# Another order of the steps of a fused decoder layer, on every engine of the core

## The chip, the core and the metric

The kernel runs on one core of a Trainium2 chip. A core has five engines with a queue of instructions each: TensorE (PE in the profile; PEld is its loading of weights), VectorE (DVE), ScalarE (ACT), GpSimd (POOL) and SyncE (SP), which here issues all DMAs. Each engine works off its own queue strictly in order, and waits at an instruction until the semaphores that it names have reached their values. The metric is the time of one execution on the device in microseconds (us); of several runs the median is given.

## What is computed

A decoder layer in float32 over 8 sequences (batches) of 256 tokens with 128 channels: linear attention, causal cross attention to a context, and a feed-forward part with routed experts and a short convolution. Each part takes a layer norm of its input and adds its output to it.

```python
def layer(x, ctx):                       # (8, 256, 128) each
    x = x + attn(layernorm(x))           # 16 heads of 8; phi(t) = elu(t) + 1
    x = x + xattn(layernorm(x), ctx)     # 16 heads of 8, causal softmax
    return x + ffn(layernorm(x))

def attn(x):
    q, k, v = split(x @ Wqkv.T); q, k = phi(q), phi(k)
    kv, k_sum = einsum('bnhd,bnhm->bhdm', k, v), k.sum(1)
    return (q @ kv / (q @ k_sum + 1e-6)) @ Wproj.T + bproj

def xattn(x, ctx):
    q, k, v = x @ Wq.T, ctx @ Wk.T, ctx @ Wv.T
    return softmax(where(causal, q @ k.T / sqrt(8), -inf)) @ v @ Wo.T

def ffn(x):                              # scores: 8 experts, two chosen
    scores = sigmoid(x @ Wr); cw = weights_of_top2(scores + router_bias)
    routed = sum(cw[e] * ((silu(x @ Wg[e]) * (x @ Wu[e])) @ Wd[e]) for e in range(4))
    routed += (cw[4] + cw[6]) * x + cw[7] * relu(x)
    return routed + causal_conv4(x, conv_w) + conv_b
```

## The kernel before

The eight batches go through the same steps, and the steps of up to four batches are mixed, so that every engine has work while others wait. A step is a Python function that issues a few instructions on one engine with the waits they need; the table `ORDER` at the head of the file lists for each engine its steps as `name.batch.number`, and `program` issues them in that order. Nothing else orders the work: neither the tiles nor the eight PSUM banks are chosen by it.

The steps, by the names that the texts below use:

- Linear attention: `stats1`, `var1` (DVE), `rstd1` (POOL, two instructions at L480 and L488), `norm1` (POOL at L498; DVE for batches 0 and 1), `self_x_t` (PE transposes), `xnT` (ACT copy), `self_q1`, `self_kv` (PE), `act_q`, `act_kv` (ACT), `phi_q`, `phi_k` (DVE), `self_sum` (PE), `kvsum` (DVE), `self_out` (PE), `div1` (DVE, three parts), `self_o_t` (PE), `o1T` (ACT), `self_proj` (PE), `x1` (DVE, adds what POOL's `bias` made). They go through `self_bank`, for batches 1 and 2 through `pv_bank` and `ffn_bank`.
- Cross attention, its operands: `stats2` to `norm2`, `cross_norm_t`, `x2nT`, `cross_q2` for q, `cross_k_v` for k and v. q and k are split into three bfloat16 parts, `hi` and `mid` (ACT), `rest` (DVE), `lo` (POOL), which SP's DMAs stack into `qs` and `ks`.
- Cross attention, its maxima: for each batch six units, `max.b.0` to `max.b.5` on PE write scores to the pair of banks `max_pair`, and `reduce` (DVE, L839) takes the maxima from it. There is one such pair, so a `max` waits for the `reduce` before it. After three units `maxrow` (PE) transposes the maxima, `max_hi` (ACT) and `max_mid` (DVE) split them, and `send_max` (SP) moves them into `qs`.
- Cross attention, softmax: `soft` (PE, six units, through `soft_pair`) needs the maxima; `exp` (ACT), `mask` (POOL, L524), `pv` (PE, two halves of three masks each), `outT`, `out_t`, `div2` (DVE), `o2_t`, `o2T`, `o_proj` (PE), `x2` (DVE).
- Feed-forward: `stats3` to `shift3` (DVE) and `norm3` (ACT, L606), `ffn_x_t`, `x3T`, `ffn_router`, `tanh_r`, `sig`, `route` (DVE, seven parts), `ffn_gate_up` (PE, two halves), `tanh_g` (ACT), `gate` and `times_up` (DVE), `hid` (POOL), `ffn_hid_t`, `hidT`, `tap` (convolution), `ffn_down` (PE, twelve products, needs `hidT` and all taps), `skip`, `relu7`, `base` (POOL), `finish` (DVE), `store_out`.

## Time and profile before

| | us |
|---|---|
| median of 3 runs (196.34 to 197.08) | 196.93 |
| the profiled execution | 196.06 |
| its span on the core | 194.3 |
| DVE busy | 163.4 |
| PE busy | 166.0 |
| ACT busy | 124.9 |
| POOL busy | 113.8 |

The span reaches from the first to the last instruction. An engine's busy time is the time in which it worked on an instruction; PE's ends are modelled. Of the views, the windows give busy times of a stretch, the timeline the instructions in order with the idle time before each and what ended it, and the granted clock is the share of TensorE's full speed. In the timelines steps of one name can be told apart by their tiles (`negmax<-max_pair` is a `reduce`) and by their time.

### The profile page before, as it was taken

Reading aid. Unit: us, or ns where it says so; the run is one execution under the profiler, and the core shown is the slowest. Engines: PE = TensorE matmul, PEld = TensorE weight load, DVE = VectorE, ACT = ScalarE, POOL = GpSimd, SP = SyncE. Lnnn points to the kernel's source line nnn. Section 1 sums busy time; section 2 is a strip of 40 time slices with the busy share of each in tenths; the row PEclk is TensorE's granted clock in tenths of the full one; section 3 lists DMA queues with packets and bytes.
Section 4 is the critical chain, followed back from the end, with each engine's and each line's share of the span. In section 5 each row is a group of like instructions: output and inputs, shape, how many; then the busy total and the mean of one; then the engine's idle time right before and its main releaser. Section 6 shows DMA issues by size and latency. Waiting matters only on the chain.

```text
span 194.3 us, 5501 instructions
## 1 busy us (share of the span) xinstructions
PE 166.0 (85%) x1812; PEld 114.5 (59%) x1812; DVE 163.4 (84%) x458; ACT 124.9 (64%) x281; POOL 113.8 (59%) x204
## 2 busy tenths in 40 slices
PE   6958697778898899995999999988988998797973
PEld 6846484545566556672866576656646546554542
DVE  6665878847787889998999989999999799399893
ACT  2036563528857798785776398858976568756560
POOL 7864877951932873798236633657366167754432
PEclk9999999969999999999999999999999999999999
DMA  5931131120332210013203211232121000000001
GB/s 174 321 142 41 36 84 48 46 69 15 97 83 57 59 32 21 1 46 107 71 4 83 60 48 31 55 86 57 44 59 33 27 7 2 27 3 0 30 2 54
DMA packets 17796, 11.00 MB, mean 57 GB/s; under 512 B 2388, under 2 KB 17108, under 8 KB 17768
## 3 DMA queue, kind: packets, MB, share of 16 engines
q1 hardware_dynamic: 17768, 10.66, 18.7%
q8 instruction: 14, 0.23, 0.5%
q14 instruction: 14, 0.11, 0.2%
HBM read 3.10 MB, written 1.05 MB: 21 GB/s over the span
## 4 chain that ended last, share of the span: by engine, by line
DVE 29%; PE 23%; issue 21%; POOL 18%; ACT 6%; DVEq 1%; POOLq 0%; ACTq 0%
DVE negmax L839 7%; PE max_pair L966 4%; POOL rstd L488 4%; POOL xn L498 4%; PE ffn_bank L966 4%; PE self_bank L966 4%; PE pv_bank L966 4%; DVE convT L944 3%; ACT probs L641 3%; POOL probs L524 2%; DVE stats L735 2%; PE soft_pair L966 2%; POOL hid L533 2%; POOL vareps L480 1%; POOL xres L506 1%
## 5 line engine op out<-in xcount | busy, mean ns | idle before, releaser
L839 DVE TENSOR_REDUCE negmax<-max_pair 128x4 f32<-128x1024 f32 (+1 forms) x48 | 58.5, 1218 | 6.6 <-PE max_pair L966 6.1
L641 ACT ACTIVATE probs<-soft_pair 128x1024 f32<-128x1024 f32 x48 | 49.0, 1020 | 8.8 <-PE soft_pair L966 8.8
L524 POOL TENSOR_SCALAR_AFFINE_SELECT probs<-probs 128x512 f32<-128x512 f32 (+1 forms) x48 | 37.5, 795 | 21.8 <-ACT probs L641 21.8
L966 PE MATMUL pv_bank<-probs,vs 128*32 128x128 f32 (+1 forms) x512 | 23.7, 328 | 1.6 <-POOL probs L524 1.4
L966 PEld LDWEIGHTS pv_bank<-probs,vs 128*32 128x32 f32 x512 | 14.4, 109 | 10.6 <-POOL probs L524 3.7
L966 PE MATMUL soft_pair<-qs,ks 64*128 64x256 bf16 (+1 forms) x256 | 18.9, 247 | 1.1 <-ACT probs L641 1.0
L966 PE MATMUL max_pair<-causal,picks 64*128 64x128 bf16 (+1 forms) x192 | 15.5, 240 | 4.8 <-DVE negmax L839 3.2
L606 ACT ACTIVATE xn<-x,shift,rstd 128x128 f32<-128x128 f32 x32 | 14.0, 488 | 8.4 <-DVE shift L759 8.4
L966 PE MATMUL max_pair<-ks,qs 64*128 64x128 bf16 (+1 forms) x256 | 18.8, 245 | 0.0
L488 POOL TENSOR_TENSOR rstd<-vareps,exponent 128x2 f32<-128x2 f32 x24 | 17.4, 725 | 2.0
L533 POOL TENSOR_TENSOR hid<-hraw,cw 128x256 f32<-128x256 f32 x16 | 10.3, 649 | 13.6 <-DVE hraw L921 7.1
L966 PE MATMUL ffn_bank<-loaded,x3T 128*128 128x8 f32 (+1 forms) x52 | 17.0, 423 | 0.6 <-ACT x3T L667 0.5
L944 DVE SCALAR_TENSOR_TENSOR convT<-x3T,loaded,convT 128x256 f32<-128x256 f32 x24 | 15.3, 638 | 0.2
L966 PEld LDWEIGHTS max_pair<-causal,picks 64*128 64x128 bf16 x192 | 6.1, 95 | 14.2 <-DVE negmax L839 8.4
L966 PEld LDWEIGHTS soft_pair<-qs,ks 64*128 64x128 bf16 x256 | 8.7, 94 | 9.8 <-ACT probs L641 5.9
L480 POOL TENSOR_SCALAR vareps<-mv 128x2 f32<-128x2 f32 x24 | 5.5, 230 | 12.7 <-DVE mv L749 11.4
L514 POOL TENSOR_TENSOR qparts<-qrest,qparts 128x256 bf16<-128x256 f32 x8 | 5.6, 703 | 8.7 <-ACT qparts L623 8.7
L548 POOL TENSOR_TENSOR base<-skip,relu 128x256 f32<-128x256 f32 x8 | 6.0, 750 | 7.3 <-DVE skip L936 4.0
L966 PEld LDWEIGHTS max_pair<-ks,qs 64*128 64x128 bf16 x256 | 10.0, 95 | 0.3
L498 POOL TENSOR_SCALAR xn<-loaded,mv,rstd 128x128 f32<-128x128 f32 x12 | 9.5, 799 | 0.1
L966 PEld LDWEIGHTS ffn_bank<-loaded,x3T 128*128 128x128 f32 x52 | 7.3, 190 | 2.6 <-ACT x3T L667 1.3
L966 PE MATMUL cross_bank<-loaded 128*128 128x128 f32 (+1 forms) x48 | 8.6, 316 | 0.1
(195 smaller groups left out, 386.8 us busy)
## 6 DMA issues: line engine op xcount, KB each, us to landing
ks<-kparts SPq DMA_DIRECT2D x48, 64.0 KB, 2.0
qs<-qparts SPq DMA_DIRECT2D x48, 64.0 KB, 2.1
out_dram<-result SPq DMA_DIRECT2D x8, 128.0 KB, 1.8
loaded<-packed_dram SPq DMA_DIRECT2D x1, 768.0 KB, 7.7
loaded<-packed_dram SPq DMA_DIRECT2D x1, 640.0 KB, 8.8
qs<-maxparts SPq DMA_DIRECT2D x32, 4.0 KB
loaded<-packed_dram SPq DMA_DIRECT2D x1, 462.5 KB, 6.3
...
```

Source lines behind the costliest of these rows:

```text
L480: nc.gpsimd.tensor_scalar(t["vareps"][:, :], t["mv"][b.par][:, :, 1], 1.0, 1e-5, ALU.mult, ALU.add).then_inc(vareps_done[n], 1)
L488: nc.gpsimd.tensor_tensor(t["rstd"][b.par][:, :], t["vareps"][:, :], exponent[:, :], ALU.pow).then_inc(rstd_done[n], 1)
L498: nc.gpsimd.tensor_scalar(t["out"][b.par][:, i, :], x_of(b)[:, i, :], t["mv"][b.par][:, i, 0:1], t["rstd"][b.par][:, i:i + 1], ALU.subtrac ...
L514: nc.gpsimd.tensor_tensor(parts[n][b.par][:, 2, :], rest[n][b.par][:, :], parts[n][b.par][:, 1, :], ALU.subtract).then_inc(lo_done[n], 1)
L524: nc.gpsimd.affine_select(out=v, in_=v, compare_op=ALU.is_ge, fill=0.0, base=0, pattern=[[0, n], [1, P]], channel_multiplier=-1).then_inc( ...
L533: nc.gpsimd.tensor_tensor(hid[b.par][:, t, :].rearrange("p (e i) -> p e i", e=EM), hid0[:, t, :].rearrange("p (e i) -> p e i", e=EM), cw[b ...
L548: nc.gpsimd.tensor_tensor(base[b.par][:, :, :], skip[b.par][:, :, :], relu7[b.par][:, :, :], ALU.add).then_inc(base_done, 1)
L606: nc.scalar.activation(t["out"][b.par][:, i, :], source[:, i, :], ACT.Identity, bias=t["shift"][b.par][:, i:i + 1], scale=t["rstd"][b.par] ...
L641: nc.scalar.activation(probs[b.par][g][:, k, :], soft_pair[:, :], ACT.Exp).then_inc(exp_done, 1)
L839: nc.vector.tensor_reduce(maxima, max_pair[:, :].rearrange("p (u h k) -> p u h k", u=2, h=n), AX.X, ALU.max, negate=True).then_inc(max_rea ...
L944: nc.vector.scalar_tensor_tensor(out=convT[b.par][:, :], in0=x3T[b.par][:, j:j + S], scalar=w["conv"][:, j:j + 1], in1=convT[b.par][:, :], ...
L966: return nc.tensor.matmul(out, lhsT, rhs, start=start, stop=stop, skip_group_check=True)
```

## The change

The table `ORDER` is replaced by another for all five engines, found with shorter occupancies (the time that a step is taken to hold its engine) for the groups of TensorE. The steps, their instructions, tiles and banks are the same. The new table is a line shorter, so POOL's code stands one line higher in the file. One wait is new, in ACT's `norm3`; the diff shows it with a line of the table for POOL and for PE.

```diff
 ORDER = {
...
     "pool": """
...
-        mask.0.5 lo_k.3.0 mask.1.0 mask.1.1 mask.1.2 rstd3.0.0 rstd1.6.0 mask.1.3 rstd2.4.0 mask.1.4 lo_q.3.0
...
+        lo_k.2.0 lo_k.3.0 rstd1.6.0 norm1.5.0 norm1.6.0 rstd3.0.0 bias.6.0 mask.1.0 lo_q.3.0 mask.1.1 mask.1.2
...
     "pe": """
...
-        self_out.3.0 max.0.1 cross_q2.1.0 max.0.2 self_o_t.3.0 cross_k_v.2.0 maxrow.0.0 self_proj.3.0 max.0.3
...
+        max.0.1 cross_q2.1.0 self_out.3.0 max.0.2 cross_k_v.2.0 maxrow.0.0 max.0.3 self_o_t.3.0 self_proj.3.0
...
                         if n == 3:
                             act.wait_ge(skip_done, b.count(2, -2))
+                            act.wait_ge(relu7_done, b.count(2, -2))
```

Three places of the order follow, two on PE and one on POOL.

PE, batch 0's linear attention between `self_sum.0` (`vones0,phik0`) and `self_proj.0` (`o1T0` into `self_bank`). `ident,xn1_0` into `ffn_bank` are the transposes of batch 2, `kvsum0,phiq0` is `self_out.0`, `ident,o10` is `self_o_t.0`. Before:

```order
L966 MATMUL self_bank<-vones0,phik0 128x144 x2
L970 MATMUL pv_bank<-ident,xn1_1 128x128 x2
L970 MATMUL ffn_bank<-ident,xn1_0 128x128 x2
L966 MATMUL self_bank<-kvsum0,phiq0 128x144 x2
L966 MATMUL pv_bank<-xnT1,loaded 128x256
L966 MATMUL ffn_bank<-xnT0,loaded 128x256
L970 MATMUL self_bank<-ident,o10 128x128 x2
L966 MATMUL pv_bank<-loaded,xnT1 128x256 x2
L966 MATMUL self_bank<-loaded,o1T0 128x128 x2
```

Now:

```order
L966 MATMUL self_bank<-vones0,phik0 128x144 x2
L970 MATMUL pv_bank<-ident,xn1_1 128x128 x2
L966 MATMUL self_bank<-kvsum0,phiq0 128x144 x2
L966 MATMUL pv_bank<-xnT1,loaded 128x256
L970 MATMUL ffn_bank<-ident,xn1_0 128x128 x2
L970 MATMUL self_bank<-ident,o10 128x128 x2
L966 MATMUL ffn_bank<-xnT0,loaded 128x256
L966 MATMUL self_bank<-loaded,o1T0 128x128 x2
```

`self_out.0` and `self_q1.1` have moved ahead of batch 2's transposes, and `self_proj.0` ahead of `self_kv.1`.

PE, between `max.0.3` (the first two rows) and `max.0.5` (the last `causal,picks` and `ks0,qs0`). `ident,xn1_0` into `self_bank` is `self_x_t.4`, `ident,xn2_0` is `cross_norm_t.2`, the single `soft_pair` row `soft.0.0`. Before:

```order
L966 MATMUL max_pair<-causal,picks 128x4x64 x4
L966 MATMUL max_pair<-ks0,qs0 128x128 x8
L970 MATMUL cross_bank<-ident,xn2_0 128x128 x2
L970 MATMUL self_bank<-ident,xn1_0 128x128 x2
L966 MATMUL max_pair<-causal,picks 128x2x64 x4
L966 MATMUL max_pair<-ks0,qs0 128x256 x4
L966 MATMUL cross_bank<-x2nT0,loaded 128x256
L966 MATMUL self_bank<-xnT0,loaded 128x256
L966 MATMUL soft_pair<-qs0,ks0 128x256 x4
L966 MATMUL max_pair<-causal,picks 128x2x64 x4
L966 MATMUL max_pair<-ks0,qs0 128x256 x4
```

Now:

```order
L966 MATMUL max_pair<-causal,picks 128x4x64 x4
L966 MATMUL max_pair<-ks0,qs0 128x128 x8
L970 MATMUL self_bank<-ident,o11 128x128 x2
L966 MATMUL self_bank<-loaded,o1T1 128x128 x2
L966 MATMUL max_pair<-causal,picks 128x2x64 x4
L966 MATMUL max_pair<-ks0,qs0 128x256 x4
L970 MATMUL self_bank<-ident,xn1_0 128x128 x2
L966 MATMUL soft_pair<-qs0,ks0 128x256 x4
L970 MATMUL cross_bank<-ident,xn2_0 128x128 x2
L966 MATMUL max_pair<-causal,picks 128x2x64 x4
L966 MATMUL max_pair<-ks0,qs0 128x256 x4
```

`max.0.4` has moved ahead of the transposes of batches 2 and 4, `soft.0.0` too, and `cross_q2.2` and `self_q1.4` behind `max.0.5`.

POOL, from `lo_k.3` (`kparts1`) on. `probs10` and `probs11` are masked in `mask.1.0` to `mask.1.5`, `rstd3_0` is `rstd3.0`, `xn1_1` and `xn1_0` are `norm1.5` and `norm1.6`. Before:

```order
L514 TENSOR_TENSOR kparts1<-krest1,kparts1 128x256
L524 AFFINE_SELECT probs10<-probs10 128x4x128 x2
L524 AFFINE_SELECT probs10<-probs10 128x1024
L480 TENSOR_SCALAR vareps3<-mv3_0 128x2
L488 TENSOR_TENSOR rstd3_0<-vareps3,exponent 128x2
L480 TENSOR_SCALAR vareps1<-mv1_0 128x2
L488 TENSOR_TENSOR rstd1_0<-vareps1,exponent 128x2
L524 AFFINE_SELECT probs11<-probs11 128x4x128
L480 TENSOR_SCALAR vareps2<-mv2_0 128x2
L488 TENSOR_TENSOR rstd2_0<-vareps2,exponent 128x2
L524 AFFINE_SELECT probs11<-probs11 128x4x128
```

Now:

```order
L513 TENSOR_TENSOR kparts1<-krest1,kparts1 128x256
L479 TENSOR_SCALAR vareps1<-mv1_0 128x2
L487 TENSOR_TENSOR rstd1_0<-vareps1,exponent 128x2
L497 TENSOR_SCALAR xn1_1<-loaded,mv1_1,rstd1_1 128x128 x2
L497 TENSOR_SCALAR xn1_0<-loaded,mv1_0,rstd1_0 128x128 x2
L479 TENSOR_SCALAR vareps3<-mv3_0 128x2
L487 TENSOR_TENSOR rstd3_0<-vareps3,exponent 128x2
L505 TENSOR_TENSOR xres0<-loaded 128x256
L523 AFFINE_SELECT probs10<-probs10 128x4x128
L513 TENSOR_TENSOR qparts1<-qrest1,qparts1 128x256
L523 AFFINE_SELECT probs10<-probs10 128x4x128
L523 AFFINE_SELECT probs10<-probs10 128x1024
```

`norm1.5`, `norm1.6`, `rstd3.0` and `bias.6` (`xres0`) now stand ahead of the first mask of batch 1. At the end of PE's queue the four transposes of `ffn_hid_t.7` now stand ahead of `ffn_down.6` instead of behind it.

## Rows read from the trace of the kernel before

**Rows 1.** Windows: length; busy us (count) of PE, PEld, DVE, ACT, POOL; clock, DMA share, GB/s.

```profile
0.00:31.39 31.39, 23.94 (x142) 19.82 (x142) 21.82 (x73) 14.32 (x40) 22.62 (x60) 1.00 0.39 128
31.39:62.25 30.86, 25.65 (x294) 16.68 (x294) 23.14 (x49) 18.46 (x41) 17.68 (x29) 0.94 0.22 60
62.25:77.47 15.22, 14.52 (x196) 9.38 (x191) 13.81 (x38) 12.56 (x27) 9.51 (x16) 1.00 0.14 36
77.47:161.76 84.29, 77.40 (x981) 52.29 (x981) 79.52 (x209) 61.27 (x133) 47.59 (x74) 1.00 0.17 47
161.76:194.30 32.54, 24.51 (x211) 16.30 (x207) 25.15 (x95) 18.25 (x41) 16.36 (x26) 1.00 0.06 18
sum 194.30, PE 166.02 PEld 114.46 DVE 163.44 ACT 124.86 POOL 113.75; mean PE 33.20 PEld 22.89 DVE 32.69 ACT 24.97 POOL 22.75
```

**Rows 2.** Timeline, TensorE, 14.9 to 15.3 us: start, duration, operation [idle before <- releaser].

```profile
14.96 0.44 PE L970 MATMUL ffn_bank<-ident,xn 128*128 128x128 f32 x2 [1.28 <-POOL xn L498]
15.23 0.66 PE L966 MATMUL self_bank<-kvsum,phiq 128*128 128x144 f32 x4
```

**Rows 3.** Timeline, VectorE, 13.5 to 16 us: kvsum.0, div1.0.

```profile
13.50 0.31 DVE L792 TENSOR_TENSOR kvsum<-self_bank,headmask 128x144 f32<-128x144 f32 x1 [0.33 <-PE self_bank L966]
15.92 0.19 DVE L800 TENSOR_SCALAR den<-self_bank 128x32 f32<-128x32 f32 x1 [2.12 <-PE self_bank L966]
```

**Rows 4.** Timeline, VectorE: reduce.0.4 and reduce.0.5.

```profile
40.98 1.23 DVE L839 TENSOR_REDUCE negmax<-max_pair 128x4 f32<-128x1024 f32 x1 [1.42 <-PE max_pair L966]
...
44.17 1.22 DVE L839 TENSOR_REDUCE negmax<-max_pair 128x4 f32<-128x1024 f32 x1 [1.81 <-PE max_pair L966]
```

**Rows 5.** Timeline, TensorE, at 40 us: self_x_t.4.

```profile
40.01 0.44 PE L970 MATMUL self_bank<-ident,xn 128*128 128x128 f32 x2 [1.19 <-POOL xn L498]
```

**Rows 6.** Windows, as in rows 1: the stretch of lower granted clock.

```profile
40.70:44.10 3.40, 3.40 (x20) 1.83 (x16) 1.38 (x3) 1.11 (x3) 0.98 (x2) 0.50 0.37 98
```

**Rows 7.** Timeline, VectorE, end: shift3.5, x2.6, finish.7.

```profile
165.57 0.62 DVE L759 SCALAR_TENSOR_TENSOR shift<-mv,rstd 128x2 f32<-128x2 f32 x1
...
169.59 0.42 DVE L870 TENSOR_TENSOR x<-pv_bank,x 128x256 f32<-128x256 f32 x1 [2.90 <-PE pv_bank L966]
...
191.60 0.42 DVE L952 TENSOR_TENSOR result<-max_pair,base 128x256 f32<-128x256 f32 x1 [0.61 <-PE max_pair L966]
```

**Rows 8.** Chain that ended last (start, duration, step): ffn_hid_t.7 and ffn_down.7.

```profile
188.11 0.67 PE ffn_bank L1168 x4
...
189.44 1.62 PE max_pair L966 x12
```

**Rows 9.** Timeline, POOL, 64 to 74 us: rstd3.0, masks, lo_q.3, bias.

```profile
64.75 0.19 POOL L480 TENSOR_SCALAR vareps<-mv 128x2 f32<-128x2 f32 x1
65.02 0.69 POOL L488 TENSOR_TENSOR rstd<-vareps,exponent 128x2 f32<-128x2 f32 x1
...
69.56 0.64 POOL L524 TENSOR_SCALAR_AFFINE_SELECT probs<-probs 128x512 f32<-128x512 f32 x1 [1.14 <-ACT probs L641]
70.17 0.67 POOL L514 TENSOR_TENSOR qparts<-qrest,qparts 128x256 bf16<-128x256 f32 x1
...
71.10 1.09 POOL L524 TENSOR_SCALAR_AFFINE_SELECT probs<-probs 128x1024 f32<-128x1024 f32 x1
72.16 1.42 POOL L506 TENSOR_TENSOR xres<-loaded 128x256 f32<-128x256 f32 x2
```

**Rows 10.** Timeline, TensorE: pv.1.1.

```profile
72.25 1.51 PE L966 MATMUL pv_bank<-probs,vs 128*32 128x256 f32 x32
```

**Rows 11.** convT: source view with min/median/max; group of lines with sum and mean.

```profile
L944 DVE SCALAR_TENSOR_TENSOR convT<-x3T,loaded,convT x24: 440/486/1251, 85.3 to 188.4; 128x256 f32<-128x256 f32 x24
...
L944 DVE SCALAR_TENSOR_TENSOR convT<-x3T,loaded,convT 128x256 f32<-128x256 f32 x24 | 15.3, 638 | 0.2
```

**Rows 12.** Timelines of VectorE and POOL at 88.5 us: shift3.1 beside mask.2.5.

```profile
88.56 1.03 DVE L759 SCALAR_TENSOR_TENSOR shift<-mv,rstd 128x2 f32<-128x2 f32 x1 [0.78 <-POOL rstd L488]
...
88.48 1.09 POOL L524 TENSOR_SCALAR_AFFINE_SELECT probs<-probs 128x1024 f32<-128x1024 f32 x1
```

More of the change, by code:

```diff
@@ L55 @@
+        mask.7.4 sig.5.0 rstd3.6.0 mask.7.5 hid.5.0 hid.5.1 rstd3.7.0 sig.6.0 base.5.0 sig.7.0 hid.6.0 hid.6.1
         hid.7.0 hid.7.1 base.6.0 base.7.0
@@ new lines @@
+        route.0.1 reduce.2.3 route.0.2 phi_k.5.0 route.0.3 route.0.4 shift2.4.0 reduce.2.4 kvsum.5.0 gate.0.0
+        reduce.2.5 route.0.5 route.0.6 times_up.0.0 skip.0.0 div1.5.0 div1.5.1 max_mid.2.1 div2.1.0 div1.5.2
+        div2.1.1 reduce.3.0 skip.0.1 rest_q.4.0 reduce.3.1 x2.1.0 x1.5.0 reduce.3.2 stats3.1.0 gate.0.1
+        stats2.5.0 var3.1.0 times_up.0.1 max_mid.3.0 var2.5.0 tap.0.1 reduce.3.3 shift2.5.0 tap.0.2 reduce.3.4
+        div2.2.0 rest_k.5.0 tap.0.3 reduce.3.5 shift3.1.0 phi_k.6.0 phi_q.6.0 div2.2.1 max_mid.3.1 finish.0.0
@@ new lines @@
+        self_x_t.6.0 maxrow.3.0 pv.2.0 max.3.3 pv.2.1 max.3.4 self_q1.6.0 out_t.2.0 ffn_hid_t.0.0 max.3.5
+        soft.3.0 self_kv.6.0 ffn_down.0.0 maxrow.3.1 self_sum.6.0 soft.3.1 max.4.0 cross_norm_t.5.0 ffn_x_t.1.0
+        self_out.6.0 o2_t.2.0 soft.3.2 max.4.1 ffn_router.1.0 o_proj.2.0 self_o_t.6.0 soft.3.3 max.4.2
+        ffn_gate_up.1.0 self_proj.6.0 maxrow.4.0 cross_q2.5.0 self_x_t.7.0 max.4.3 soft.3.4 self_q1.7.0
+        ffn_gate_up.1.1 max.4.4 soft.3.5 self_kv.7.0 cross_k_v.6.0 max.4.5 soft.4.0 pv.3.0 soft.4.1
```

208 lines of the change are left out of this document (98 added, 110 removed).

## The prediction

> **What bounds the kernel now.** I read the page's busy times first, then the windows by stage, then in the timelines what stands behind the waits of VectorE (DVE) and TensorE (PE). The profiled execution took 196.06 us, its span was 194.3, and the median of the runs shown is 196.93, 0.87 above it. An order takes no instruction away, so I count the idle time of the engine that works most: DVE is busy 163.44 of 194.3 us, PE 166.02 [rows 1]. Subtracting DVE's busy time from each stage of [rows 1] gives its idle time: 9.6 us before the first reduce of scores, 7.7 from there to the first reduce of batch 2 (31.39 to 62.25), 1.4 to that of batch 3 (77.47), 4.8 in the following 84.3 us to the end of the last reduce, 7.4 behind it (5.1 to the end of the last addition and 2.3 of the last store). In the long middle DVE is 94% and PE 92% busy: there an order can win little, and lose. What it can win lies in the first 62 us, where the pipeline over batches fills, and at the end.
>
> **The start, up to the first reduce.** PE's transposes of batch 2 (self_x_t.2) waited 1.28 us for POOL's norm1.2 and began at 14.96; self_out.0, behind them in the queue, began at 15.23 [rows 2]. Its last input, kvsum.0, was done at 13.50 + 0.31 = 13.81, and DVE stood 2.12 us before div1.0 [rows 3]. Now self_out.0 goes ahead of self_x_t.2, so up to 15.23 - 13.81 = 1.4 us of batch 0's chain go. What is late next: on ACT the copy xnT.2 still stands ahead of o1T.0, and norm1.2 comes some 0.6 later, because var1.2 now stands behind phi_k.0. Following batch 0 step by step through the new queues with the durations of before (projection, norm 2, the q projection, the three parts of q, about 2 us of DMA), I get the first reduce at about 30.55 instead of 31.39: 0.85 kept of 1.4. The bounds are 0 and 1.4; I take 0.85, since max.0.0 no longer stands behind self_sum.3. Of the 0.85, 0.2 is DVE work now put behind this reduce, so the idle time saved is **0.65**. The DVE memsets and POOL constants that change places here lie under PE's 18 warm-up products, whose end holds the first transposes back in either order.
>
> **Batch 0's fourth to sixth reduce, up to 62 us.** reduce.0.4 waited 1.42 us for max.0.4, and reduce.0.5 1.81 us for max.0.5 [rows 4]. Ahead of both in PE's queue stood self_x_t.4, which waited 1.19 us for POOL's norm1.4 [rows 5]. From 40.7 to 44.1, behind these waits, PE's granted clock was 0.50 (the 1.2 GHz level); half of the 3.4 us it was busy then, 1.7, is the most that this cost [rows 6]. Now max.0.4 stands ahead of self_x_t.4, and norm1.4 ahead of rstd2.2 and lo_q.1 on POOL; soft.0.0 moves up with them. Then reduce.0.4 follows x1.3 almost at once and max.0.5 fits under it: the two waits of 3.23 us go, save some 0.3. Whether the clock still falls elsewhere I cannot read; PE has fewer waits ahead of it, so I take it as not falling, and 1.7 is the price if it does. Some comes back: between max.0.5 and max.1.0 there are now 4.2 us of PE work, 2.2 before. Following the queues on, I get reduce.1.0 2.65 us early and reduce.2.0 at about 58.6, 3.65 early, with 0.8 us less DVE work ahead of it: 2.85 of idle time saved in all, **2.2** of it here (bounds: 0.5, if the clock falls again, and 3.2).
>
> **SP's queue.** Of the moved steps' DMAs, lo_q.1, lo_k.1 and mid_q.1 stand behind send_max.0.0 and so behind max_mid.0.0, at about 36.5; they have some 7 us to land before max.1.0 needs them. store_out.0 now stands behind send_max.3.1 and ahead of send_max.4.0, where finish.0 follows max_mid.3.1 on DVE, so nothing waits for it. I cost SP at nothing.
>
> **62 to 162 us.** Up to reduce.3.0 the new order puts 1.2 us more DVE work and holds POOL up (first rival); I get it at about 76.35, 1.1 early, thus 1.1 + 1.2 = 2.3 of idle time saved: **0.55 given back**. From there to the last reduce I add, unit by unit, the larger of PE's and DVE's work between two score tiles: from batch 2 on it is 99.7 us before and 100.4 after, no difference that carries weight. So the remaining 4.8 us of idle stay: **0** (bounds: 2.4 won, if half of it goes; 2.3 lost, if all that was won is used up).
>
> **The end.** DVE waited 2.90 us before x2.6, for o_proj.6 [rows 7]. shift3.5 ended at 166.19, behind div2.6 and skip.4; it now stands ahead of div2.6, so norm3.5 and exp.7.3 on ACT can begin some 0.7 earlier, and o_proj.6 goes ahead of ffn_router.5. That brings x2.6 about 1.2 and x2.7 about 1.1 us earlier. What is late next is PE: x_t.7 stands behind ffn_down.5, only 0.4 earlier. And at the very end ffn_hid_t.7 now stands ahead of ffn_down.6: before, ffn_down.6 was over when hid_t.7 began at 188.11 [rows 8], now both ffn_down (1.6 us each) follow it. hid_t.7 itself can begin at about 187.0. So ffn_down.7 ends only 0.2 earlier, and the 0.61 us that finish.7 waited beyond its neighbour [rows 7], for base.7, shrink to nothing: **0.7** (bounds -0.9, if hid_t.7 is no earlier, and 1.2).
>
> **The added wait** of norm3 for relu7 of two batches before is for a step earlier in ACT's own queue, at the nearest with hidT and two tanh_g between: nothing waits, and nothing queued behind it is held.
>
> **Sum.** 0.65 + 2.2 - 0.55 + 0 + 0.7 = 3.0 us. The profiled execution would take 196.06 - 3.0 = 193.1; the median 196.93 - 3.0 = **193.9**.
>
> **Rivals.** *POOL holds PE up (slower).* Ahead of batch 1's masks POOL now has norm1.5, norm1.6, rstd3.0 and bias.6, and rstd3.0 waits for DVE's var3.0. From var3.0's end to the last mask of batch 1 there are then rstd3.0, rstd2.4, rstd1.7 (0.96 each), bias.6 (0.71), four masks of 0.64, two of 1.09, lo_q.3 (0.67) and sig.0: 9.2 us of work [rows 9]. pv.1.1 needs that mask, and behind it on PE are maxrow.2.1 and max.3.0, so DVE's reduces. pv.1.1 began at 72.25 before [rows 10] and has 1.4 us more PE work ahead of it now, so 73.65 is the point of no gain: it is passed when var3.0 ends after 64.4. Before it ended at 64.15; I expect 61.75, since x2.0 is early. If it ended at 66.5, as when o_proj.0 waits and the clock falls again, the front would cost 2.1 instead of winning: 196.93 + 2.1 - 0.7 = 198.3. Against it speaks the 2.6 us of room.
>
> *What was won is used up (no change).* PE and DVE are over 90% busy in the middle, and a queue made for shorter PE steps makes DVE wait wherever a step takes longer than thought. If 2.3 of the 2.3 go, the end's 0.7 is left: 196.2.
>
> *POOL and DVE meet more often.* DVE's convT step took 486 ns in the median, 638 in the mean, 1251 at most [rows 11]; a shift of 147 ns at best took 1.03 us from 88.56 on, while POOL's mask ran from 88.48 to 89.57 [rows 12]. In convT alone that is 24 x 152 ns = 3.6 us. The order changes which steps meet; if such meetings were to double, 193.9 + 3.6 = 197.5, and if half went, 192.1. The Trainium skill, page "SBUF — State Buffer", section "SBUF: two separate sides", says that DVE and GpSimd share a port pair under an exclusive lock, held for a whole instruction. By that rule each new pairing stretches the later one to the end of the first, and the sum would stay open by as much; the row of the shift agrees with it, which ended within 0.02 us of the mask.
>
> *More is won.* If half of the middle's 4.8 us of idle goes as well, 191.5.
>
> **How the numbers follow.** About 0.5%, 1 us, is what a measurement of this kernel can tell from no change. Forecast (192 to 195.9): 0.60. More won (190.8 to 192): 0.13. Used up, or meetings (196 to 197.9): 0.17. Slower by over 0.5% (POOL holding PE, or doubled meetings with nothing kept): 0.10. So faster 0.73, same 0.17, slower 0.10. The range leaves out half of each end: 191.2 to 197.4.
>
> **What would show it.** In the trace after: the first reduce at 30.3 to 30.9 us, that of batch 2 at 58 to 60, no wait of over 0.5 us before the second and third reduce of batch 0's second half, granted clock 1.00 from 7 us on; DVE's idle 5 us in the first 31 to 60 us instead of 7.7; pv.1.1 without a wait for POOL; hid_t.7 and both ffn_down in one row at the end. It is wrong if the first reduce of batch 3 begins after 77.5, or if DVE idles over 7 us from there to the last reduce.

## The result, and the profile of the kernel after

The kernel after takes 189.54 us in the median of four runs (188.86 to 190.57), the kernel before 196.63 beside it: a ratio of 0.966, with a 95% interval from 0.958 to 0.974. Forecast were 193.9 and a range from 191.2 to 197.4. The sign was right; of the gain of 7.1 us the forecast had 3.0.

The profiled run took 188.86 us, with a span of 187.1. The windows by stage, with the columns of [rows 1], cut at the first reduce, at the first of batch 2, at the first of batch 3, at the last, and at the end:

```profile
0.00:29.94 29.94, 23.09 (x139) 18.80 (x140) 21.32 (x73) 14.52 (x41) 22.41 (x61) 1.00 0.42 135
29.94:57.35 27.41, 23.29 (x281) 15.17 (x281) 22.66 (x47) 17.31 (x39) 19.42 (x31) 1.00 0.22 60
57.35:74.69 17.34, 16.49 (x209) 11.42 (x210) 15.95 (x47) 15.13 (x33) 10.87 (x18) 1.00 0.16 42
74.69:153.34 78.65, 76.04 (x951) 51.35 (x955) 74.47 (x201) 59.08 (x126) 45.59 (x69) 1.00 0.19 51
153.34:187.10 33.76, 25.49 (x239) 16.87 (x236) 25.33 (x94) 19.56 (x44) 16.71 (x27) 1.00 0.06 17
sum 187.10, PE 164.40 PEld 113.62 DVE 159.73 ACT 125.59 POOL 115.00; mean PE 32.88 PEld 22.72 DVE 31.95 ACT 25.12 POOL 23.00
```

The same stretch of the kernel before, from the start of batch 3's first reduce to the start of the last one (the fourth stage of [rows 1] ends with that reduce, 1.2 us later):

```profile
77.47:160.54 83.07, 76.18 (x953) 51.55 (x957) 78.30 (x207) 60.09 (x131) 47.08 (x74) 1.00 0.17 48
```

Stage by stage, the kernel after wins 1.45 us up to the first reduce (31.39 to 29.94), 3.45 from there to batch 2 (30.86 to 27.41), gives 2.12 back up to batch 3 (15.22 to 17.34, with 2.0 us more PE work moved in), wins 4.42 in the long middle (83.07 to 78.65), and nothing behind the last reduce (33.76 in both). The sum is 7.2.

The fourth row is the surprise. The same 76 us of PE work, but DVE is busy 74.47 us instead of 78.30. Some 1.8 us of this difference are work that now stands ahead of the stretch: up to batch 3 DVE's busy time grew from 58.77 to 59.93 us, although steps became shorter there too, and six fewer DVE instructions lie in the stretch. The rest are instructions that became shorter. Over the whole span, where both kernels run the same instructions, DVE is busy 159.73 us instead of 163.44. The forecast took DVE's work as a constant. Which instructions became shorter, the groups of lines show; in the kernel after (line, operation, shape, count | busy us, mean ns | idle before):

```profile
L944 DVE SCALAR_TENSOR_TENSOR convT<-x3T,loaded,convT 128x256 f32<-128x256 f32 x24 | 13.4, 564 | 0.1
L936 DVE SCALAR_TENSOR_TENSOR skip<-xn,cskip,x 128x128 f32<-128x128 f32 x16 | 4.8, 341 | 0.0
L759 DVE SCALAR_TENSOR_TENSOR shift<-mv,rstd 128x2 f32<-128x2 f32 x16 | 4.2, 261 | 0.6 <-POOL rstd L487 0.5
```

and in the kernel before (its convT is in [rows 11], 638 ns in the mean):

```profile
L936 DVE SCALAR_TENSOR_TENSOR skip<-xn,cskip,x 128x128 f32<-128x128 f32 x16 | 5.8, 404 | 0.1
L759 DVE SCALAR_TENSOR_TENSOR shift<-mv,rstd 128x2 f32<-128x2 f32 x16 | 5.1, 316 | 2.5 <-POOL rstd L488 2.5
```

An instruction such as convT, 0.44 us at best, is longer in many of the places where it begins inside an instruction of POOL; it then ends just after that one (the last section counts which). I set every DVE instruction against the lower quartile of its kind: before has 30 that are longer by over 0.08 us, 12.05 us in sum; after has 21, 7.9 us. The difference of 4.1 answers to the 3.7 that DVE's busy time lost (where two instructions overlap on DVE, as the halves of norm1.0 do, the sum counts a delay twice). By stage the sums are 2.2 us up to batch 3, 6.3 in the middle and 3.5 behind the last reduce in before, and 1.3, 4.3 and 2.4 in after.

**PE's clock, in all runs.** The mean granted clock of a run comes in steps: one fall to the 1.2 GHz level, some 3.4 us long, takes about 0.009 from it. Of 59 runs of the kernel before, one was at 1.000 with 195.1 us, 12 at 0.991 with 195.8 in the mean, 34 at 0.982 or 0.983 with 196.9, 10 at 0.974 with 197.7, and two lower. Eight runs of the kernel after: 188.9 and 189.3 at 0.998 to 1.000, 188.9 in the mean of four at 0.989 to 0.991, 190.6 and 190.7 at 0.982. So a fall costs about 0.9 us; at an equal clock the new order is worth 6.0 to 6.9 us, and the rest of the 7.1 is that it has a fall less in most runs. Below, runs are compared at an equal clock where the medians mix.

### The profile page after: what moved, and what is told of

Read it like the earlier page. It is cut to its first block, busy times and chain, and to the rows that moved or that the text cites. A ratio compares the mean times of both kernels' runs of the same rounds, so it can differ in the third digit from the quotient of the medians.

```text
span 187.1 us, 5507 instructions
## 1 busy us (share of the span) xinstructions
PE 164.4 (88%) x1812; PEld 113.6 (61%) x1812; DVE 159.7 (85%) x458; ACT 125.6 (67%) x281; POOL 115.0 (61%) x204
## 4 chain that ended last, share of the span: by engine, by line
PE 32%; issue 22%; DVE 15%; POOL 12%; SPq 8%; DMA 4%; ACT 4%; POOLq 0%; DVEq 0%; ACTq 0%
SPq L372 7%; PE max_pair L966 7%; PE soft_pair L966 5%; PE ffn_bank L966 5%; DVE negmax L839 5%; PE pv_bank L966 5%; POOL hid L532 3%; POOL probs L523 3%; PE self_bank L966 3%; DMA qs<-qparts 3%; PE cross_bank L966 2%; POOL rstd L487 2%; DMA ks<-kparts 2%; POOL xn L497 1%; SPq L387 1%
## 5 line engine op out<-in xcount | busy, mean ns | idle before, releaser
L966 PE MATMUL max_pair<-causal,picks 64*128 64x128 bf16 (+1 forms) x192 | 15.3, 238 | 7.4 <-DMA qs<-qparts 2.5
L487 POOL TENSOR_TENSOR rstd<-vareps,exponent 128x2 f32<-128x2 f32 x24 | 18.3, 761 | 2.0
L944 DVE SCALAR_TENSOR_TENSOR convT<-x3T,loaded,convT 128x256 f32<-128x256 f32 x24 | 13.4, 564 | 0.1
L479 POOL TENSOR_SCALAR vareps<-mv 128x2 f32<-128x2 f32 x24 | 6.0, 249 | 11.3 <-DVE mv L749 9.7
L540 POOL TENSOR_SCALAR sig<-tanr 128x16 f32<-128x16 f32 x8 | 1.6, 203 | 16.6 <-ACT tanr L683 16.6
## 6 DMA issues: line engine op xcount, KB each, us to landing
loaded<-packed_dram SPq DMA_DIRECT2D x2, 192.0 KB, 2.9
```

The lines of the kernel that those rows point to most:

```text
L479: nc.gpsimd.tensor_scalar(t["vareps"][:, :], t["mv"][b.par][:, :, 1], 1.0, 1e-5, ALU.mult, ALU.add).then_inc(vareps_done[n], 1)
L487: nc.gpsimd.tensor_tensor(t["rstd"][b.par][:, :], t["vareps"][:, :], exponent[:, :], ALU.pow).then_inc(rstd_done[n], 1)
L944: nc.vector.scalar_tensor_tensor(out=convT[b.par][:, :], in0=x3T[b.par][:, j:j + S], scalar=w["conv"][:, j:j + 1], in1=convT[b.par][:, :], ...
L966: return nc.tensor.matmul(out, lhsT, rhs, start=start, stop=stop, skip_group_check=True)
```

## The experiments

**The middle by halves.** Orders glued from both: every engine takes one kernel's order up to a point and then the other's, without the steps it has already run. The third batch's first reduce is reduce.2.0.

```
front_new:  after up to the third batch's first reduce | before
front_old:  before up to there                         | after
tail_old:   after up to the last reduce                | before
tail_new:   before up to there                         | after
```

> Every engine takes the new order up to about the third batch's first reduce (57 us in the profile of after) and the old order from there. My theory of the result: 3.9 us of DVE's idle time are won up to that reduce and kept, and the other 3 us are DVE work that got shorter in the middle, where DVE and POOL meet in other places. Then reduce.2.0 begins at about 57.4, DVE's idle time up to the last addition is about 25 us as in after, and DVE's busy time stays near before's 163 (within 1.5, since the meetings of the old middle return, shifted): about 192 us, 4 to 5 under before. Rival, the old middle eats the lead (the rival 'won is used up' of the prediction): reduce.2.0 early, the last reduce no earlier than in before, 195 to 197. Rival, the front is all of it: 189.5.

Measured: 192.77 us, ratio 0.978 (0.970 to 0.985). reduce.3.0 began 3.82 us earlier than in before, and the last addition 3.80 earlier: the lead goes through the old order of the middle untouched. DVE was busy 162.4 us up to the start of the last addition, 163.0 in before (all such sums below end there). The theory held, and the rival by which the middle eats the lead fell.

> The old order up to the third batch's first reduce, the new one behind it. By my theory the front's 3.9 to 4.9 us of lead are missing and the shorter DVE work of the middle (2 to 3 us) stays: about 193.5 to 195, with DVE busy near 160.5 and idle near 29. If the lead of the middle hangs on the front too (the meetings of DVE and POOL depend on when each gets there, not only on the order), DVE is busy near 163 and the time is near 196.5. If the front is worth nothing of its own, 190.

Measured: 195.12 us, ratio 0.989 (0.978 to 1.001); one of its four runs took 261.38 us at a granted clock of 0.562, and the other three 193.84 to 195.99. The stretch from reduce.3.0 to the last reduce took 78.18 us, with DVE busy 74.42, as in after, though it began 5.9 us later than there. So the shorter DVE work belongs to the order of the middle, not to the lead with which it is reached. All profiles say the same: in seven with the old order of the middle and nothing else changed there, it takes 83.0 to 83.7 us; in five with the new one, 78.1 to 78.7. (The profiled run had three falls of the clock, two of them between 30 and 50 us; at 0.990 it took 193.84, 2 below before.)

> The new order up to the last reduce, the old one behind it. The two profiles show the last addition 7.21 us earlier than in before and the last reduce 7.21 earlier too, so the new tail gave no time in sum. Theory: the same as after, within 0.7 us (188.8 to 190.2). Rival, the prediction's own sum for the end (0.7 won by hid_t.7 ahead of ffn_down.6 and by norm3.5 earlier): 0.7 slower than after, 190.2. Other rival: the new tail cost time, which the lead hid: 188.5 or less.

Measured: 189.23 us, ratio to before 0.958 (0.950 to 0.966): the same as after. From the last reduce to the last addition it needed 32.19 us, with a fall of the clock in that stretch, and after 31.05; the front of that run was 0.6 faster.

> The old order up to the last reduce, the new one behind it. Theory: within 0.5 us of before (196.1 to 197.1), with hid_t.7 ahead of ffn_down.6 but no earlier end, since DVE meets POOL elsewhere. The prediction's sum: 0.7 faster, 196.2, and in the trace x2.7 1.1 us and hid_t.7 1.1 us earlier against the last reduce than in before.

Measured: 195.5 us, ratio 0.993 (0.988 to 0.997). Against the last reduce, x2.6 came 1.06 us earlier than in before (forecast 1.2), x2.7 0.79 (forecast 1.1), norm3.7 on ACT 0.65, and x_t.7 on PE 0.13 later: there the gain ends. The last addition was 0.05 earlier.

What holds x_t.7 is to be read in the kernel after. Timeline of TensorE, ffn_x_t.7 and ffn_hid_t.7:

```profile
174.98 0.41 PE L970 MATMUL ffn_bank<-ident,xn 128*128 128x128 f32 x2 [0.88 <-DVE result L952]
...
180.88 0.66 PE L1168 MATMUL ffn_bank<-ident,hid 128*128 128x128 f32 x4 [2.06 <-POOL hid L532]
```

and of VectorE ahead of it, route.6.3 and finish.5:

```profile
173.29 0.61 DVE L894 SCALAR_TENSOR_TENSOR wsel<-picked,sig 128x16 f32<-128x16 f32 x1
...
174.43 0.40 DVE L952 TENSOR_TENSOR result<-ffn_bank,base 128x256 f32<-128x256 f32 x1
```

x_t.7 writes the bank that finish.5 reads. finish.5 follows ffn_down.5 (end 174.10) in both kernels and stands behind other steps on DVE, one of them, 0.16 us at best, lengthened to 0.61. An earlier norm3.7 is worth nothing while the bank is taken. And hid_t.7 waited 2.06 us for POOL's hid.7.1, so standing ahead of ffn_down.6 won it nothing either.

**The masks left out.** POOL's mask on 8 columns of one head instead of 128 of all:

```
-  v = probs[b.par][g][:, k, :].rearrange("p (n q) -> p n q", n=n)[:, :, 0:P]
+  v = probs[b.par][g][:, k, :].rearrange("p (n q) -> p n q", n=n)[:, 0:1, 0:8]
...
-  pattern=[[0, n], [1, P]], ...
+  pattern=[[0, 1], [1, 8]], ...
```

> The kernel before, with the causal mask put on 8 columns of one head instead of all 128 of all heads: the masking is left out, so POOL's 48 masks are almost nothing, and all else is unchanged. Theory: a DVE instruction that meets a POOL instruction runs on to that instruction's end. The rows of before show 30 DVE instructions lengthened so, 12.05 us in sum, about 7 us of it beside masks. So DVE's busy time falls from 163.4 to about 157 (155 to 159). Rival, the lengthening is DVE's own (a slow start of some shapes, or waits for the write of an earlier result): DVE's busy time stays within 1 us of 163.4. The time itself falls by the same or more, since PE's waits for masks go too.

> The kernel after, with the same masking left out. Theory: 7.9 us of lengthened DVE instructions in after, about 4 of it beside masks, so DVE's busy time falls from 159.7 to about 155.5 (154 to 157), and the difference of the two kernels in DVE's busy time shrinks from 3.7 to about 1. Rival, DVE's work is shorter in after for another reason than POOL: the difference stays at 3 to 4 us.

Measured: 190.7 us and 187.5 (185.9 and 189.2). Up to the last addition DVE was busy 156.7 instead of 163.0 in the one, 155.8 instead of 159.3 in the other: 6.3 and 3.5 us less without touching DVE, and the difference of the two orders went from 3.7 to 0.9. So 2.8 of the 3.7 us go with the masks. One of the meetings, tap.3.1. Timeline of VectorE and POOL in the kernel before:

```profile
144.15 1.10 POOL L524 TENSOR_SCALAR_AFFINE_SELECT probs<-probs 128x1024 f32<-128x1024 f32 x1
144.38 1.15 DVE L944 SCALAR_TENSOR_TENSOR convT<-x3T,loaded,convT 128x256 f32<-128x256 f32 x1
```

and of nomask_before, at the same place of the order:

```profile
140.39 0.20 POOL L524 TENSOR_SCALAR_AFFINE_SELECT probs<-probs 128x8 f32<-128x8 f32 x1
140.62 0.48 DVE L944 SCALAR_TENSOR_TENSOR convT<-x3T,loaded,convT 128x256 f32<-128x256 f32 x1
```

And the middle as a whole, windows of nomask_before:

```profile
76.61:156.01 79.40, 75.67 (x953) 51.70 (x957) 74.07 (x207) 60.04 (x131) 30.30 (x74) 1.00 0.18 50
```

The old order with 4.2 us less DVE work needs 79.40 us for the middle instead of 83.07. Leaving out the masks also ends waits of PE for POOL. In the middle of before these were one of 1.1 us for a mask and one of 0.4 for another step; here 0.2 us is left, so by these waits some 1.3 of the 3.67 us at most can be that. In nomask_after the middle took 78.82, against 78.65 in after, though DVE was busy 2.4 us less: there less DVE work was worth nothing.

**The kernel after again, and with fewer meetings.**

> The kernel after once more, unchanged, as the measure for the three runs beside it. 189.5 by the runs so far (188.9 to 190.6, the higher ones at a lower mean granted clock). If the lengthened DVE instructions are set by the order, its DVE is again busy 159.7 us (within 0.2) with the same 20 or so lengthened steps, whatever the clock does.

Measured: 188.76 us, ratio 0.960 (0.954 to 0.966). The profiled run had two falls of the clock, one ahead of reduce.0.4 and one at ffn_gate_up.7; the end took 1.2 us longer. DVE was busy 159.15 up to the last addition (159.31 in the first profile), with 20 lengthened steps instead of 21, 7.5 us. So the meetings are the order's; they change little with where the clock falls.

```
 ORDER["dve"]
-  shift3.0 reduce.2.2            ->  reduce.2.2 shift3.0
-  route.0.0 route.0.1 reduce.2.3 ->  reduce.2.3 route.0.0 route.0.1
-  skip.0.0 div1.5.0 div1.5.1     ->  div1.5.0 div1.5.1 skip.0.0
-  tap.0.1 reduce.3.3, phi_k.7 reduce.4.5, tap.2.1 rest_q.6,
-  tap.3.1 stats3.4 reduce.6.4, shift3.4 finish.3.0,
-  shift3.6 gate.5.0 times_up.5.0 ->  each behind the steps that followed it
```

> The kernel after with nine steps of DVE one to two places later, nothing else: shift3.0, route.0.0 (with route.0.1 behind it), skip.0.0, tap.0.1, phi_k.7, tap.2.1, tap.3.1, shift3.4 and shift3.6, each of which read two SBUF tiles and ran on to the end of a POOL instruction in after; now a step goes ahead of it whose input lies in PSUM or which has one input. Theory (only DVE steps with two SBUF inputs are held by POOL, and the order alone decides which): in the rows of after those nine are 3.9 us too long in sum; at their new places POOL's instruction is over or nearly so, and some 2.5 to 3 of that go, so DVE is busy about 157 and the time is 1.5 to 3 us below the kernel after beside it. Rival: the steps behind them move up by as much and meet other POOL instructions, DVE's busy time stays within 1 us of 159.7 and the time the same within 0.7.

Measured: 192.64 us, ratio to before 0.978 (0.973 to 0.984); at 0.989 to 0.991 it took 191.7 to 192.0, after 188.9: 3 us slower. DVE lost the work as expected (157.15 up to the last addition, 2.2 less; 14 lengthened steps, 5.3 us), and idled 7.0 us more, in a run with three falls of the clock. Where it began, the timelines of fix_after show: VectorE, shift3.0 and what waited after it,

```profile
62.90 0.62 DVE L759 SCALAR_TENSOR_TENSOR shift<-mv,rstd 128x2 f32<-128x2 f32 x1
...
65.68 0.28 DVE L846 TENSOR_TENSOR maxparts<-max_pair,maxparts 16x128 bf16<-16x128 f32 x1 [1.49 <-ACT maxparts L647]
...
68.49 1.23 DVE L839 TENSOR_REDUCE negmax<-max_pair 128x8 f32<-128x1024 f32 x1 [1.74 <-PE max_pair L966]
```

and TensorE, ffn_x_t.0, then the window behind it:

```profile
64.48 0.61 PE L970 MATMUL ffn_bank<-ident,xn 128*128 128x128 f32 x2 [1.81 <-ACT xn L606]
```

```profile
64.50:68.20 3.70, 3.70 (x21) 3.01 (x23) 1.07 (x5) 2.48 (x9) 1.67 (x5) 0.54 0.03 8
```

shift3.0, moved by one reduce, met another POOL instruction all the same (0.62 us), and it is not free to come later: ACT's norm3.0 waits for it, PE's ffn_x_t.0 for that (1.81 us), and max.2.3 stands behind ffn_x_t.0. Behind the wait PE's clock fell to 0.54. That is 2.7 us lost at reduce.2.3. In the middle, where five of the other moves lie, the stretch took 79.24 us with DVE busy 72.96, against 78.65 with 74.47: nothing won, as in nomask_after.

```
 ORDER["dve"]
-  ... shift2.0 ... shift3.7 (16 steps)
 rstd on POOL, for norm 2 and 3
+  nc.gpsimd.tensor_scalar(shift, mv[:, :, 0], -1.0, 0.0, ALU.mult, ALU.add)
   nc.gpsimd.tensor_tensor(rstd, vareps, exponent, ALU.pow)
+  nc.gpsimd.tensor_tensor(shift, shift, rstd, ALU.mult)
```

> The kernel after with the 16 shifts (-mean times rstd, 128x2) of the second and third normalisation taken from DVE: POOL computes them in two small instructions beside rstd, in the same order otherwise. Theory: DVE loses 16 x 0.15 us = 2.4 and the 1.6 us by which four of them are too long in after, and the waits for rstd that stood ahead of them (2.5 us in before): DVE busy about 156, POOL busy 6 to 7 us more, time 186.5 to 188.5. Rival: POOL's rows are longer by 0.4 us for each normalisation, norm2, norm3 and the masks come that much later, and PE waits for POOL: no faster than the kernel after, or up to 2 us slower.

Measured: 191.71 us, ratio to before 0.971 (0.964 to 0.978); 191.1 to 191.7 at 0.989 to 0.991, 2.5 us slower than after. The profiled run, with three falls of the clock, took 193.19. At the last reduce it was 0.1 us ahead of after, with DVE busy 1.7 us less and idle 1.6 more; all the loss lies behind it: finish.5 came 1.0 later, and PE's clock was low in the stretch that ends the kernel. What the 2.5 us of the runs with one fall are, no profile shows. Windows of shift_pool:

```profile
175.00:180.00 5.00, 3.60 (x9) 2.23 (x10) 3.84 (x19) 0.78 (x3) 1.35 (x3) 0.68 0.09 28
180.00:185.00 5.00, 3.61 (x12) 2.20 (x11) 4.13 (x12) 2.24 (x7) 2.27 (x3) 0.50 0.00 0
```

**Who holds the middle.** Three kernels with less DVE work than after won nothing there, so PE is the suspect: 12 extra products, the same in both orders.

```
 def soft_scores(b, u):
+    if 3 <= b.c <= 6 and u % 2 == 0:
+        warm(1)      # one product of 128 columns, overwritten by what follows
```

> The kernel before with one extra product of 128 columns (0.24 us each in the rows of the run with extra products at the front) ahead of every second soft.b.u of batches 3 to 6 on PE, 12 in all, 2.9 us, whose results are overwritten. In before PE is busy 76.2 of the 83.1 us from the first reduce of batch 3 to the last one, DVE 78.3. Theory (DVE holds this stretch in before): the stretch grows by 0 to 1 us. Rival (PE holds it there too): it grows by 2.5 to 3.

> The same 12 extra products in the kernel after, where PE is busy 76.0 of the 78.65 us of this stretch and DVE 74.5. Theory (with fewer lengthened DVE instructions PE holds the stretch, so that a further cut of DVE's work gives nothing): the stretch grows by 2 to 3 us, and the kernel is 2 to 3 us slower than after. Rival (DVE or the lockstep of both holds it): it grows by 0 to 1, as in before.

Windows of the middle, midfill_before, then midfill_after:

```profile
78.17:163.26 85.09, 80.74 (x977) 54.48 (x981) 78.19 (x207) 60.75 (x131) 47.35 (x74) 1.00 0.17 47
```

```profile
74.05:155.79 81.74, 80.75 (x975) 54.47 (x979) 75.02 (x200) 59.35 (x127) 45.76 (x70) 1.00 0.18 49
```

PE's busy time grew by 4.6 and 4.7 us (more than the 2.9 I had worked out), the stretch by 2.0 in before and by 3.1 in after; the kernels took 197.57 us (ratio to before 1.003, 1.000 to 1.006) and 192.75. At 0.988 to 0.991 that is 1.8 more than before and 3.5 more than after. For after the theory held, a little above its 2 to 3 us: PE is left idle 1.0 of 81.74 us. For before it missed: I had expected up to 1 us. DVE does not hold the old order alone; its 6.9 us of idle PE time took up 2.5 of the extra 4.6.

The middle in one table, us from the first reduce of batch 3 to the last reduce:

| kernel | length | PE busy | DVE busy |
|---|---|---|---|
| before | 83.07 | 76.18 | 78.30 |
| before, masks left out | 79.40 | 75.67 | 74.07 |
| after | 78.65 | 76.04 | 74.47 |
| after, masks left out | 78.82 | 75.84 | 72.08 |
| after, nine steps moved | 79.24 | 76.04 | 72.96 |
| after, shifts on POOL | 78.66 | 75.88 | 73.55 |
| before, extra PE work | 85.09 | 80.74 | 78.19 |
| after, extra PE work | 81.74 | 80.75 | 75.02 |

In the order of after the length stays at PE's 76 us and 2.6 to 3.2 more, however far DVE's work falls below 74.5 (four more profiles of this order, unchanged in the middle, have 78.1 to 78.3, that is 2.2 to 2.3 more).

**The front, piece by piece.**

```
 ORDER["pe"] of before
swap_start:  -  self_x_t.1 self_x_t.2 self_out.0
             +  self_x_t.1 self_out.0 self_x_t.2
swap_max:    -  cross_norm_t.2 self_x_t.4 max.0.4 ... soft.0.0 max.0.5
             +  max.0.4 cross_norm_t.2 self_x_t.4 ... soft.0.0 max.0.5
swap_max5:   +  max.0.4 cross_norm_t.2 max.0.5 self_x_t.4 ... soft.0.0
filler:      +  fill.0.4 cross_norm_t.2 fill.0.9 self_x_t.4 max.0.4 ... max.0.5
             (fill: that many products into soft_pair)
```

> The kernel before with self_out.0 ahead of self_x_t.2 on PE, the step from which the prediction worked out the earlier start. The prediction's sum: self_out.0 begins at 13.8 to 13.9 instead of 15.23, and the first reduce 0.85 (0 to 1.4) earlier than 31.39. Rival: self_x_t.2 and batch 2's chain behind it come later by as much and hold the first reduce by another way, 0 to 0.3 earlier. The two profiles show 1.46 for all the changes of the start together, 0.6 of it DVE's norm1.0, which no longer meets POOL's clearing of tiles; here that part stays, so with the theory 0.85 and not 1.46.

Measured: 196.41 us, ratio 0.995 (0.991 to 0.999). self_out.0 began at 13.32, the first reduce at 30.61 instead of 31.39: 0.78 earlier, as summed up (0.85). The lead was there unchanged at x2.6 (0.86); in the profiled run a fall of the clock behind it took it away. At an equal clock the runs are 0.4 to 1.3 faster.

> The kernel before, with max.0.4 ahead of cross_norm_t.2 and self_x_t.4 in PE's queue, one of the two places on which the front's gain is put. Theory: reduce.0.4 goes from 40.98 to about 39.6, its wait of 1.42 us gone, reduce.0.5 about 1 us earlier; PE's clock still falls behind self_x_t.4, which waits as long for norm1.4; at the third batch's first reduce 0.5 to 1.4 us of lead are left, and the time is 0.3 to 1.4 under before. Rival: the lead is lost by reduce.1.0, since max.0.5 still stands behind self_x_t.4; within 0.3 us of before.

Measured: 195.06 us, ratio 0.990 (0.987 to 0.992). reduce.0.4 came 1.38 earlier, reduce.0.5 0.48, and these 0.48 were there at the end (0.17 of them are from ahead of this place). Timeline of VectorE in swap_max, reduce.0.4, reduce.0.5 and reduce.1.0:

```profile
39.60 1.23 DVE L839 TENSOR_REDUCE negmax<-max_pair 128x4 f32<-128x1024 f32 x1 [0.21 <-PE max_pair L966]
43.69 1.22 DVE L839 TENSOR_REDUCE negmax<-max_pair 128x4 f32<-128x1024 f32 x1 [2.71 <-PE max_pair L966]
...
46.71 1.22 DVE L839 TENSOR_REDUCE negmax<-max_pair 128x8 f32<-128x1024 f32 x1 [0.19 <-PE max_pair L966]
```

The wait moved by one reduce, from 1.42 and 1.81 us [rows 4] to 0.21 and 2.71.

> The kernel before with max.0.4 ahead of cross_norm_t.2 and max.0.5 ahead of self_x_t.4 on PE, nothing else: both products of batch 0's second half that DVE waited for no longer stand behind the wait for norm1.4. With max.0.4 alone reduce.0.4 came 1.4 earlier and reduce.0.5 only 0.5, PE's clock still falling between the two. Theory of the prediction (the waits for the products are what the front is worth): reduce.0.5 at about 41 instead of 44.17, reduce.1.0 1 to 2.6 earlier than 47.19, the same lead at the last reduce, and the time 1 to 2.5 under before. Rival (the clock is worth most of it, and PE's work behind takes the rest back): reduce.1.0 at most 0.8 earlier and the granted clock again at 0.5 for about 3.4 us near 41 us.

Measured: 195.22 us at a clock of 1.000 (before 195.09), 198.7 in three runs at 0.974 (before 197.7): nothing won. Timeline of VectorE, reduce.0.5 and reduce.1.0, and a window:

```profile
41.60 1.23 DVE L839 TENSOR_REDUCE negmax<-max_pair 128x4 f32<-128x1024 f32 x1 [0.45 <-PE max_pair L966]
48.90 1.22 DVE L839 TENSOR_REDUCE negmax<-max_pair 128x8 f32<-128x1024 f32 x1 [1.43 <-PE max_pair L966]
```

```profile
44.00:48.00 4.00, 2.88 (x13) 1.46 (x13) 0.94 (x3) 3.35 (x7) 0.00 (x0) 0.50 0.01 2
```

reduce.0.5 comes 2.6 us early and reduce.1.0 1.7 late: what stood between the two products now stands behind both and ahead of max.1.0, soft.0.0 and exp.0.0 with it, and the clock falls there.

> The kernel before, with 4 extra products ahead of cross_norm_t.2 and 9 ahead of self_x_t.4 on PE, whose results nobody reads, so that PE has work in the two waits at 38 to 40 us behind which its granted clock fell to 0.50. The order and all waits stay. If the front's gain is above all the clock, it stays at 1.00 from 40 to 44 us, reduce.1.0 comes 0.5 to 1.7 us earlier than 47.19, and the time falls by about as much. If the gain is the waits that went, reduce.1.0 stays within 0.3 of 47.19, or later, as the extra products themselves stand ahead of max.0.4.

Measured: 196.71 us, ratio 0.998 (0.995 to 1.001). The window in which before had 0.50 [rows 6], and one further up, in the profiled run of filler:

```profile
14.00:18.00 4.00, 3.33 (x11) 2.83 (x12) 1.43 (x5) 1.32 (x4) 2.57 (x8) 0.59 0.06 17
...
40.70:44.10 3.40, 3.40 (x32) 2.46 (x30) 1.24 (x3) 0.76 (x2) 1.91 (x4) 1.00 0.25 65
```

Behind the extra products the clock stayed up. They stand ahead of max.0.4 themselves, so at an equal clock the kernel is 0.8 to 1.3 us slower; that four of nine runs had no fall at all (of before one in 59) brings it level. In this run the clock fell at 14 us instead, as it did in the profile of tail_new, whose front is before's word for word: from reduce.0.4 to reduce.0.5 that one needs 1.83 us, before 3.19. So the fall at 41 us cost 1.36 us there.

**A little more.**

```
 ORDER["pe"] of after
+  ... ffn_down.5 fill.7.3 ffn_x_t.7 fill.7.1 ffn_router.7 ... ffn_hid_t.6 fill.7.6 ffn_hid_t.7 ...
```

> The kernel after with 3, 1 and 6 extra products on PE ahead of ffn_x_t.7, ffn_router.7 and ffn_hid_t.7, in three waits of 0.88, 0.46 and 2.06 us at the end; nobody reads their results. In the second profile of after PE's clock fell to 0.54 between 177 and 181 us behind these waits, and the last reduce's lead of 0.6 us too little became 1.8 at the end. Theory: the extra products (0.25 us each) fit into the waits and the clock does not fall there, so the time is that of the best runs of after, 188.4 to 189.0, with less spread. Rival: they hold up the transposes behind them or the clock falls elsewhere: 189 to 190.5.

Measured: 188.56 us (187.17 to 189.42), ratio to before 0.958 (0.953 to 0.962). Five of six runs had a clock of 0.999 or 1.000, of after two of eight one of 0.998 or 1.000. Windows at the end, after2, then after_warm:

```profile
177.00:181.00 4.00, 4.00 (x9) 1.62 (x8) 2.67 (x15) 1.08 (x4) 1.90 (x4) 0.57 0.01 2
```

```profile
174.00:181.00 7.00, 6.31 (x41) 4.57 (x39) 6.64 (x29) 3.55 (x10) 2.79 (x6) 1.00 0.07 21
```

From the last reduce to the last addition it takes 31.04 us, as the first profile of after without a fall there, 32.27 in after2. It is the fastest of the kernels run, but its interval overlaps with that of after, so a gain over after is not shown; that the fall at the end is gone, is (the one fall of the profiled run lies at 31 us).

## Point by point: why the forecast had the sign and not the size

**The whole sum.** The forecast counted idle time of DVE up to the last addition: 3.0 us were to be saved, and 3.5 were (28.6 to 25.1). That this total came so near is in part luck, since 4.5 us were saved up to the last reduce, where the stages of the forecast add up to 2.3, and 1.0 was lost behind it, where 0.7 was to be won. The other 3.7 us of the gain are DVE's busy time, which the forecast put at nothing. The step that failed is its premise, "An order takes no instruction away, so I count the idle time of the engine that works most": it holds the busy time of that engine constant.

**The start: right, and short by DVE work.** Forecast was the first reduce at 30.55, it came at 29.94 (in seven other profiles of the new start at 29.6 to 30.6). The step from which it was worked out held alone (0.78 of the 0.85). Of what came on top, 0.3 is DVE work that was taken as fixed: norm1.0, 1.02 us long from 5.86 on beside POOL's clearing of a tile in before, takes 0.70 us from 5.14 on now. And kvsum.0, with self_out.0 and div1.0 behind it, came 0.7 earlier than summed up. Timeline of TensorE and VectorE in after, self_out.0 and div1.0, the answers to [rows 2, 3]:

```profile
13.18 0.76 PE L966 MATMUL self_bank<-kvsum,phiq 128*128 128x144 f32 x4
```

```profile
13.97 0.19 DVE L800 TENSOR_SCALAR den<-self_bank 128x32 f32<-128x32 f32 x1 [0.52 <-PE self_bank L966]
```

**Up to 62 us: right, a little low.** Forecast were 2.85 us of idle time saved up to reduce.2.0, measured 3.92 (3.6 in front_new). The answers to [rows 4] in after, reduce.0.4, reduce.0.5 and reduce.1.0:

```profile
38.45 1.23 DVE L839 TENSOR_REDUCE negmax<-max_pair 128x4 f32<-128x1024 f32 x1
...
40.27 1.23 DVE L839 TENSOR_REDUCE negmax<-max_pair 128x4 f32<-128x1024 f32 x1 [0.21 <-PE max_pair L966]
...
43.99 1.23 DVE L839 TENSOR_REDUCE negmax<-max_pair 128x8 f32<-128x1024 f32 x1 [0.83 <-PE max_pair L966]
```

The two waits went as forecast, 0.83 came back. The argument had it by the waits alone; the single moves show that this place works only as a whole. One product ahead shifts the wait by one reduce, two products ahead lose it all again at max.1.0, and only with norm1.4 earlier on POOL, soft.0.0 moved up and less between does the lead stay. How much each of those last moves gives was not tried. And part of the 3.9 is the fall of the clock, 1.36 us in this profile: runs of front_new without a fall are 2.3 to 2.8 us below the one such run of before. The price of 1.7 stood in the prediction as a possible loss; it was a gain that I had not counted.

**62 us to batch 3: right in kind.** 0.55 us of idle time given back was forecast; none was (3.92 to 3.94). reduce.3.0 came at 74.69, 1.7 before the forecast, all of it from ahead.

**POOL holding PE up: fell.** var3.0 ended at 60.11, 4.3 us before the point from which that rival decides, and pv.1.1 began at 69.94 without a wait.

**The middle: here the forecast failed most.** The step was "I add, unit by unit, the larger of PE's and DVE's work between two score tiles", 99.7 us against 100.4, so 0. The DVE durations in that sum were those of the profile before, with 7.1 us of lengthening from batch 2 to the last reduce inside them, and I carried them over into the new order as if a step kept its length wherever it stood; the new order has 5.5 us of it there. Of the 4.42 us by which the middle itself became shorter, 0.6 is idle time, some 2.0 are shorter steps, and some 1.8 are work moved ahead of it, which the forecast had seen (1.2 us) and which made the stage ahead longer. The rival of meetings named the mechanism, and was mis-sized and mis-weighted: priced by convT alone, 3.6 us, where all steps together had 12.05; given a chance of loss and none of gain beyond half of 3.6. Both rows from which it could have been sized were there: the means of [rows 11] against their medians, and the same for skip and shift. It was also no matter of chance. The meetings came with the order in every profile: 7.5 and 7.9 us in two profiles of after, 12.0 in filler, which runs before's order half a microsecond shifted; each part brought its own into the glued kernels (0.1 us up to the first reduce with the new start, 1.1 to 1.2 with the old one; 3.8 to 4.2 in the new middle, 6.0 in the old one; 2.4 with the new end, 2.7 and 3.5 with the old one).

**Why not more.** With fewer meetings, and with DVE work moved ahead of it, PE holds the middle: busy 76.04 of 78.65 us. A sum by engines would have shown the floor: the old order could win at most 83.07 - 76.2 = 6.9 us there. 4.4 were won, as some 2.6 us of PE's time stay idle in the new order. Behind the last reduce DVE's busy time is 1.0 us shorter too (26.4 to 25.3), and its idle time 1.0 longer: there the shorter steps bought nothing.

**The end: failed.** 0.7 was forecast, 0 measured. x2.6 and x2.7 came earlier as worked out; the step that failed is "What is late next is PE: x_t.7 stands behind ffn_down.5, only 0.4 earlier". It stands behind finish.5 too, which has to empty its bank, and finish.5 had moved behind more DVE work. hid_t.7, put at 187.0, gained nothing, since POOL's hid.7.1 is no earlier.

**The rest.** The added wait of norm3, costed at nothing, shows nowhere as a wait. SP's queue, costed at nothing too, is not as clear: in after's profile PE waits 0.80 us for a DMA into ks at 74.03, just ahead of reduce.3.0, and 0.59 for one into qs at 125.64; the profile of before has no wait of PE for a DMA of over 0.3 us. Whether they cost time, no run tells. DVE's idle time from the first reduce to batch 2 was 27.41 - 22.66 = 4.75 us, forecast 5. In that profile the clock was 1.00 in every stage, as forecast, but only two of the eight runs of after had such a clock.
